# Iterated attention on one core: a round that takes two head pairs instead of one, on all engines

## The chip, the core and the metric

One core of one Trainium2 chip runs the whole kernel. It has TensorE (PE, and PEld for its weight loads), VectorE (DVE), ScalarE (ACT), GpSimd (POOL) and the queue of SyncE. The metric is device time in microseconds (us); lower is better.

## What is computed

A stack of four layers, each with an attention and a feed-forward part, on x of shape (16, 256, 128). Only the attention of the last layer is touched. It has 16 heads of 64 and repeats its own update three times:

```
q, k = layernorm(heads(x @ Wq + bq)), layernorm(heads(x @ Wk + bk)); v = heads(x @ Wv + bv)
def step(carry, _):
    q_cur, converged = carry
    scores = einsum('bhqd,bhkd->bhqk', q_cur, k) / scale
    attn = softmax(scores, axis=-1)
    out = einsum('bhqk,bhkd->bhqd', attn, v)
    diff = norm(out - q_cur)
    q_new = where(converged, q_cur, out)
    return (q_new, converged | (diff < UPDATE_STEPS_EPS)), None
(q_final, _), _ = lax.scan(step, (q, False), None, length=3)
return merged(q_final) @ Wo + bo
```

## The kernel before

`iterated_attention` works in 32 units (NU), each one sequence of 256 tokens and 8 of the 16 heads. A unit is three steps of four head pairs: 12 pairs, 384 in all (NPS). Every engine has its own instruction stream, written out by hand, and works through it in order; semaphores tie the streams together.

A pair p goes through these stages. PE: `scores(p)` (L2456), 12 fp32r matmuls in tiles of 64 rows, into banks S(p, 0) and S(p, 1), which alternate with the pair's parity. DVE: `maxima(p, e)` (L2717), one for each head e of the pair. ACT: `exps(p, e)` (L2588), two exponentials a head with their sums. DVE: `invert(p)` (L2724), both heads' sums in one reciprocal. POOL: `norm(p, e)` (L2873). PE: `turn(p, e)` (L2466), four transposes a head into bank PT(e), of which there is one for each e. ACT and DVE: `move_even` (L2596) and `move_odd` (L2730) copy PT(0) and PT(1) to SBUF. PE: `weigh(p)` (L2481), attention times V in tiles of 64 columns, into O, half of bank 6. ACT: `high(p)` rounds O to fp32r (L2609) and, in the first two steps, copies it in full as well (L2613). DVE: `low(p)` (L2736), what the rounding left. The scores of the same heads in the next step, four pairs on, need high and low.

The order of round p is, on PE: weigh(p-3), turn(p-2), scores(p), and then at most one of the things that belong to a neighbouring unit: a `product` (L2411 to L2413, the projection of x for the next unit, bank M), a `turn_p` (L2428, 4 transposes of projected k or q, right behind turn), or an `out_product` (L2512, the output projection, 12 matmuls, bank M). ACT: exps(p-1), high(p-3), move_even(p-2). DVE: maxima(p-1), the background, invert(p-1), move_odd(p-2), low(p-3). POOL: background, then norm(p-1, 0) and norm(p-1, 1). The background prepares the next unit: `add_bias`, `sum_squares`, `variance`, `newton` (L2683 to L2685), `split_q` (L2694) on DVE; `root`, `lay`, `first_high` and `square_moves` on ACT; `square`, `scale`, `split_k`, and `differ` (L2867, q after a step less q before it) on POOL.

## Time and profile before

| | |
|---|---|
| three runs, median (lowest, highest) | 3319.6 us (3316.22, 3321.14) |
| the profiled execution, first to last instruction | 3317.6 us |
| busy, of the whole span | PE 94%, DVE 78%, ACT 73%, POOL 60% |
| iterated attention | from about 1694 us to the end, half of the span |

One execution was profiled. A page gives the busy time of each engine; behind it stand the chain of work that ended last, the instructions in order of time, and busy times of chosen stretches. Matmuls overlap in the records (each is listed with its fill and drain), so PE's busy share says little on how fast it goes; the distance from the start of one block to the start of the next does.

### The profile page before, as it was taken

The numbers are of one execution on the slowest core, as the hardware profiler recorded it, in microseconds if no ns is written. First come the engines' busy times: TensorE is split into PE (matmuls) and PEld (weight loads), VectorE is DVE, ScalarE is ACT, GpSimd is POOL, SyncE is SP. The second block draws the span as 40 slices with busy tenths as digits, with TensorE's granted clock in tenths as the row PEclk, the third lists the DMA queues.
The fourth block names the chain that finished last, engine by engine and source line by source line (L and its number), as shares of the span: only waits on it lengthen the run. The fifth ranks groups of instructions, "written<-read, shape, count | busy, mean of one in ns | idle before, by whom it ended". The sixth has DMA issues, their size and how long they took to land.

```text
span 3317.6 us, 74521 instructions
## 1 busy us (share of the span) xinstructions
PE 3124.8 (94%) x25143; PEld 2376.0 (72%) x25143; DVE 2572.0 (78%) x5708; ACT 2422.7 (73%) x7208; POOL 1985.8 (60%) x1917
## 2 busy tenths in 40 slices
PE   6999999998699989999989999999999999999997
PEld 5777777766588878788867777777677776776675
DVE  7999999976877775465467787787788788778776
ACT  6888898874355557446448888888888888888885
POOL 3432323322355645425238888888888888888884
PEclk8999999998799989999989999999999999999999
DMA  3122422200000010201100000000000000000000
GB/s 115 63 64 65 127 83 78 80 17 7 1 1 1 1 49 8 71 8 30 33 13 2 2 2 1 2 2 1 2 1 2 1 2 1 2 2 1 2 2 26
DMA packets 67142, 80.44 MB, mean 24 GB/s; under 512 B 7696, under 2 KB 57936, under 8 KB 66512
## 3 DMA queue, kind: packets, MB, share of 16 engines
q1 hardware_dynamic: 65472, 75.27, 7.3%
q8 instruction: 207, 3.39, 0.4%
q14 instruction: 167, 1.37, 0.1%
q10 hardware_dynamic: 1296, 0.41, 0.1%
HBM read 56.79 MB, written 18.87 MB: 23 GB/s over the span
## 4 chain that ended last, share of the span: by engine, by line
PE 45%; POOL 6%; ACT 5%; DVE 4%; issue 3%; DVEq 0%; POOLq 0%; ACTq 0%
PE psum L2466 8%; PE psum L2481 8%; PE psum L2456 8%; PE psum L2512 5%; POOL attn_p L2873 4%; ACT attn_p L2588 3%; PE psum L2411 2%; POOL attn_qf L2867 2%; PE psum L1853 2%; PE psum L1704 2%; PE psum L1946 2%; PE psum L1706 2%; PE psum L1705 2%; PE psum L1753 1%; DVE sb_few L2717 1%
## 5 line engine op out<-in xcount | busy, mean ns | idle before, releaser
L2588 ACT ACTIVATE attn_p<-psum,sb_few 128x256 f32<-128x256 f32 x1536 | 707.8, 476 | 254.4 <-DVE sb_few L2717 249.6
L2873 POOL TENSOR_TENSOR attn_p<-attn_p,sb_few 128x512 f32<-128x512 f32 x768 | 782.4, 1039 | 135.1 <-DVE sb_few L2724 135.1
L2717 DVE TENSOR_REDUCE sb_few<-psum 128x2 f32<-128x512 f32 x768 | 491.4, 681 | 20.7 <-PE psum L2456 20.6
L2466 PEld LDWEIGHTS psum<-sb_kept,attn_p 128*128 128x128 f32 x3072 | 328.8, 141 | 164.3 <-issue 94.2
L2481 PE MATMUL psum<-attn_pt,attn_v 128*64 128x256 f32 x3072 | 416.3, 391 | 31.6 <-DVE attn_ql L2736 27.5
L2466 PE MATMUL psum<-sb_kept,attn_p 128*128 128x128 f32 x3072 | 426.9, 280 | 8.9 <-POOL attn_p L2873 8.9
L537 ACT ACTIVATE sb_a_p<-psum,sb_a_nm 128x256 f32<-128x256 f32 x1024 | 406.8, 499 | 11.3 <-DVE sb_a_nm L464 11.1
L464 DVE TENSOR_REDUCE sb_a_nm<-psum 128x2 f32<-128x512 f32 x512 | 328.4, 683 | 39.3 <-PE psum L358 25.1
L2481 PEld LDWEIGHTS psum<-attn_pt,attn_v 128*64 128x64 f32 x3072 | 192.8, 136 | 179.5 <-issue 58.2
L2588 ACT ACTIVATION_READ_ACCUMULATOR attn_p<-psum,sb_few 128x1 f32 x1536 | 318.5, 207 | 0.0
L2730 DVE COPY attn_pt<-psum 128x512 f32<-128x512 f32 x384 | 262.7, 684 | 71.2 <-PE psum L2466 68.2
L588 POOL TENSOR_TENSOR sb_a_rot<-sb_a_t 128x256 f32<-128x256 f32 x64 | 46.6, 728 | 432.1 <-DVE sb_a_t L444 431.9
L368 PE MATMUL psum<-sb_kept,sb_a_p 128*128 128x128 f32 x2048 | 277.0, 278 | 0.4
L2456 PE MATMUL psum<-attn_kh,attn_qh 64*128 64x256 f32 x1536 | 257.1, 331 | 2.8 <-DVE attn_ql L2694 2.8
L1509 POOL TENSOR_TENSOR experts_hh_low<-experts_h,experts_hh_high 128x512 fp32r<-128x512 f32 x136 | 175.8, 1293 | 133.7 <-ACT experts_hh_high L1534 133.7
L2596 ACT COPY attn_pt<-psum 128x512 f32<-128x512 f32 x384 | 239.3, 623 | 6.5 <-PE psum L2466 6.5
L368 PEld LDWEIGHTS psum<-sb_kept,sb_a_p 128*128 128x128 f32 x2048 | 219.2, 141 | 22.0 <-issue 2.5
L2724 DVE RECIPROCAL sb_few<-sb_few 128x4 f32<-128x4 f32 x384 | 67.8, 177 | 213.8 <-ACT attn_p L2588 211.2
L2456 PE MATMUL psum<-attn_kl,attn_qh 64*128 64x256 f32 x1536 | 216.7, 279 | 0.0
L2456 PE MATMUL psum<-attn_kh,attn_ql 64*128 64x256 f32 x1536 | 215.6, 277 | 0.0
L545 ACT COPY sb_a_pt<-psum 128x512 f32<-128x512 f32 x256 | 153.8, 601 | 63.4 <-PE psum L368 62.7
L1529 ACT ACTIVATE experts_sg<-psum 128x512 f32<-128x512 f32 x136 | 81.4, 598 | 153.8 <-PE psum L1590 145.2
(436 smaller groups left out, 8105.5 us busy)
## 6 DMA issues: line engine op xcount, KB each, us to landing
sb_a_spread<-a_spilled SPq DMA_DIRECT2D x96, 256.0 KB, 3.0
a_spilled<-sb_a_part_hi SPq DMA_DIRECT2D x64, 128.0 KB
a_spilled<-sb_a_part_lo SPq DMA_DIRECT2D x64, 128.0 KB
sb_a_spread<-a_spilled SPq DMA_DIRECT2D x32, 128.0 KB, 2.8
sb_gate_up<-in_L_ffn_Wg SPq DMA_DIRECT2D x32, 128.0 KB
sb_gate_up<-in_L_ffn_Wu SPq DMA_DIRECT2D x32, 128.0 KB
sb_down_w<-in_L_ffn_Wd SPq DMA_DIRECT2D x32, 128.0 KB, 2.5
sb_x<-in_L_attn_x SPq DMA_DIRECT2D x4, 512.0 KB, 7.4
```

Of the source, the lines that this page charges most:

```text
L368: mm = pe.transpose(PT(e)[:, kt * N + t * P:kt * N + (t + 1) * P], Pr[:, p % 3, e, t, kt * P:(kt + 1) * P], c.ident)
L464: dve.tensor_reduce(nm[:, p % 4, e, :], S(p, e).rearrange("p (t n) -> p t n", t=TB), AX.X, ALU.max, negate=True).then_inc(maxed.sem, 1)
L537: ins = act.activation(Pr[:, p % 3, e, t, :], S(p, e)[:, t * N:(t + 1) * N], ACT.Exp, bias=nm[:, p % 4, e, t:t + 1])
L1509: pool.tensor_tensor(hh_low[i % 3][:, :], hh[i % 3][:, :], hh_high[i % 3][:, :].bitcast(F32), ALU.subtract).then_inc(parted.sem, 1)
L2456: mm = pe.matmul(S(p, e)[:, t * N:(t + 1) * N], a_[n][half(e), hp, t * P:(t + 1) * P], b_[u % 2][half(e), hp, :], start=(n_ == 0), stop=(n ...
L2466: mm = pe.transpose(PT(e)[:, kt * N + t * P:kt * N + (t + 1) * P], Pr[p % 3][:, e, t, kt * P:(kt + 1) * P], c.ident)
L2481: mm = pe.matmul(O[half(e), :], V[u % 2][:, kt, h * HD3:(h + 1) * HD3], PTs[p % 2][:, e, kt, :], start=(kt == 0), stop=(kt == TB - 1))
L2588: ins = act.activation(Pr[p % 3][:, e, t, :], S(p, e)[:, t * N:(t + 1) * N], ACT.Exp, bias=nm[:, p % 4, e, t:t + 1], accum_out=rsum[:, p % ...
L2596: act.copy(PTs[p % 2][:, 0, :, :], PT(0).rearrange("p (k n) -> p k n", k=TB)).then_inc(even.sem, 1)
L2717: dve.tensor_reduce(nm[:, p % 4, e, :], S(p, e).rearrange("p (t n) -> p t n", t=TB), AX.X, ALU.max, negate=True).then_inc(maxed.sem, 1)
L2730: dve.tensor_copy(PTs[p % 2][:, 1, :, :], PT(1).rearrange("p (k n) -> p k n", k=TB)).then_inc(odd.sem, 1)
L2873: pool.tensor_tensor(P3, P3, spread(rinv[:, p % 4, e, :], N), ALU.mult).then_inc(normed.sem, 1)
```

## The change

The four streams are rewritten in rounds of two pairs: `TURNS` = 192 rounds, `UR` = 6 to a unit (i = 0 to 5). In round r the pairs b, b+1 with b = 2(r-2) are turned and weighed, the pairs a, a+1 with a = 2(r-1) go through maxima, exponentials and norms, and the scores of b+4, b+5 are made. O gets both halves of bank 6, one for each parity. One ACT copy rounds both pairs' outputs (`highs`), a second keeps them in full (`keep`), and waits for both lows. The sums are inverted head by head. `differ` goes in halves. `normed` and `turned` become a semaphore for each parity of head. PT(0) and PT(1) also take one product and two of the turn_p, so that turn has a further wait in three of six rounds (on add_bias or lay). The diff without the loops that it removes, which stand above, and without the helpers that place the background of ACT, DVE and POOL (which work they place in which round is told below):

```diff
-    O, M = c.banks[6][:, 0:N], c.banks[7]
+    O2 = c.banks[6].rearrange("p (h n) -> p h n", h=2)
+    O = lambda p: O2[:, p % 2, :]
+    M = c.banks[7]
     S = lambda p, e: c.banks[2 * (p % 2) + e]
     PT = lambda e: c.banks[4 + e]
     qslot = lambda u, s: (4 * u + s) % 3
     NPS = NU * ROUNDS
+    TURNS, UR = NPS // 2, ROUNDS // 2
...
-        scored, weighed, inverted = (c.steps(k, NPS) for k in ("scored", "weighed", "inverted"))
-        maxed, exped, normed, turned = (c.steps(k, 2 * NPS) for k in ("maxed", "exped", "normed", "turned"))
+        scored, weighed = (c.steps(k, NPS) for k in ("scored", "weighed"))
+        maxed, exped, inverted = (c.steps(k, 2 * NPS) for k in ("maxed", "exped", "inverted"))
+        normed, turned = ([c.steps(k + e, NPS) for e in ("", "_odd")] for k in ("normed", "turned"))
         even, odd = c.steps("even_moved", NPS), c.steps("odd_moved", NPS)
-        pair_high, pair_low = c.steps("pair_high", NPS), c.steps("pair_low", NPS)
+        pairs_high, pairs_kept, pair_low = c.steps("pair_high", TURNS), c.steps("kept", 2 * TURNS // 3), c.steps("pair_low", NPS)
...
+            def between_turns(u, i):
+                if i == 3 and u:
+                    out_product(u - 1, 2)
+                elif i == 4 and u < NU:
+                    out_product(u, 0)
+                if u + 1 < NU:
+                    if i == 0:
+                        product(u + 1, 1)
+                    elif i == 5:
+                        turn_p(u + 1, 2)
+            def behind_weighing(u, i):
+                if u + 1 < NU:
+                    if i < 3:
+                        product(u + 1, i + 2)
+                    elif i == 3:
+                        turn_p(u + 1, 0)
+                    elif i == 4:
+                        product(u + 1, 5)
+                        turn_p(u + 1, 1)
+                    else:
+                        turn_p(u + 1, 3)
+                if u + 2 < NU and i == 5:
                     product(u + 2, 0)
             def scores(p):
...
             def turn(p, e):
-                pe.wait_ge(*normed(2 * p + e))
+                pe.wait_ge(*normed[e](p))
                 if p:
                     pe.wait_ge(*(even, odd)[e](p - 1))
+                u, i = divmod(p // 2 + 1, UR)
+                if p % 2 == 0 and u + 1 < NU:
+                    if e == 0 and i == 2:
+                        pe.wait_ge(*biased(6 * (u + 1) + 4))
+                    elif e == 0 and i == 4:
+                        pe.wait_ge(*affine(4 * (u + 1) + 1))
+                    elif e == 1 and i == 5:
+                        pe.wait_ge(*affine(4 * (u + 1) + 3))
...
             def weigh(p):
...
                 pe.wait_ge(*even(p))
                 pe.wait_ge(*odd(p))
-                if p:
+                if p and p % 2 == 0:
                     pe.wait_ge(*pair_low(p - 1))
+                    u_, s_, hp_ = place(p - 2)
+                    if s_ < STEPS - 1:
+                        pe.wait_ge(*pairs_kept(4 * u_ + 2 * s_ + hp_ // 2))
                 for kt in range(TB):
                     for e in range(2):
                         h = 2 * hp + e
-                        mm = pe.matmul(O[half(e), :], V[u % 2][:, kt, h * HD3:(h + 1) * HD3],
+                        mm = pe.matmul(O(p)[half(e), :], V[u % 2][:, kt, h * HD3:(h + 1) * HD3],
                                        PTs[p % 2][:, e, kt, :], start=(kt == 0), stop=(kt == TB - 1))
...
+            for r in range(TURNS + 4):
+                u, i = divmod(r, UR)
+                p = 2 * (r - 2)
+                turning = 0 <= p < NPS
+                if turning:
+                    turn(p, 1)
+                    turn(p, 0)
+                between_turns(u, i)
+                if turning:
+                    turn(p + 1, 1)
+                    turn(p + 1, 0)
+                    weigh(p)
+                    weigh(p + 1)
+                behind_weighing(u, i)
+                if r < TURNS:
+                    scores(p + 4)
+                    scores(p + 5)
+                if i == 5:
+                    out_product(u, 1)
+                if r == TURNS + 1:
                     total(0)
...
             def exps(p, e):
                 act.wait_ge(*maxed(2 * p + e))
                 if p >= 3:
-                    act.wait_ge(*turned(2 * (p - 3) + e))
-                if p >= 4 and e == 0:
-                    act.wait_ge(*inverted(p - 4))
+                    act.wait_ge(*turned[e](p - 3))
+                if p >= 4:
+                    act.wait_ge(*inverted(2 * (p - 4) + e))
...
-            def high(p):
+            def highs(p):
                 u, s, hp = place(p)
-                act.wait_ge(*weighed(p))
+                act.wait_ge(*weighed(p + 1))
...
-                ins = act.copy(qh[qslot(u, s + 1)][:, hp, :], O)
+                act.copy(qh[qslot(u, s + 1)][:, hp:hp + 2, :], O2).then_inc(pairs_high.sem, 1)
+            def keep(p):
+                u, s, hp = place(p)
                 if s < STEPS - 1:
+                    act.wait_ge(*pair_low(p + 1))
                     if hp == 0 and u:
                         act.wait_ge(*diff_squared(2 * (u - 1) + 1))
-                    ins = act.copy(qf(u, s + 1)[:, hp, :], O)
-                ins.then_inc(pair_high.sem, 1)
+                    act.copy(qf(u, s + 1)[:, hp:hp + 2, :], O2).then_inc(pairs_kept.sem, 1)
...
+            for r in range(TURNS + 4):
+                u, i = divmod(r, UR)
+                a, b = 2 * (r - 1), 2 * (r - 2)
+                turning, rising = 0 <= b < NPS, 0 <= a < NPS
+                if i == 0 and 0 < u < NU:
+                    first_high(u, 1)
+                if rising:
+                    exps(a, 0)
+                behind_first_exps(u, i)
+                if turning:
+                    move_even(b)
+                if rising:
+                    exps(a, 1)
+                if turning:
+                    move_even(b + 1)
+                if rising:
+                    exps(a + 1, 0)
+                if i == 5 and u + 1 < NU:
+                    lay(u + 1, 2)
+                if turning:
+                    highs(b)
+                if rising:
+                    exps(a + 1, 1)
+                behind_highs(u, i)
+                if turning:
+                    keep(b)
+                behind_keep(u, i)
...
-            def invert(p):
-                dve.wait_ge(*exped(2 * p + 1))
+            def invert(p, e):
+                dve.wait_ge(*exped(2 * p + e))
                 if p >= 4:
-                    dve.wait_ge(*normed(2 * (p - 4) + 1))
-                dve.reciprocal(rinv[:, p % 4, :, :], rsum[:, p % 4, :, :]).then_inc(inverted.sem, 1)
+                    dve.wait_ge(*normed[e](p - 4))
+                dve.reciprocal(rinv[:, p % 4, e, :], rsum[:, p % 4, e, :]).then_inc(inverted.sem, 1)
...
             def low(p):
...
-                dve.wait_ge(*pair_high(p))
-                dve.tensor_tensor(ql[n][:, hp, :], O, qh[n][:, hp, :].bitcast(F32), ALU.subtract).then_inc(pair_low.sem, 1)
+                dve.wait_ge(*pairs_high(p // 2))
+                dve.tensor_tensor(ql[n][:, hp, :], O(p), qh[n][:, hp, :].bitcast(F32), ALU.subtract).then_inc(pair_low.sem, 1)
...
+            for r in range(TURNS + 4):
+                u, i = divmod(r, UR)
+                a, b = 2 * (r - 1), 2 * (r - 2)
+                turning, rising = 0 <= b < NPS, 0 <= a < NPS
+                if rising:
+                    maxima(a, 0)
+                behind_first_maxima(u, i)
+                if rising:
+                    maxima(a, 1)
+                behind_second_maxima(u, i)
+                if turning:
+                    move_odd(b)
+                if rising:
+                    invert(a, 0)
+                    maxima(a + 1, 0)
+                behind_third_maxima(u, i)
+                if turning:
+                    move_odd(b + 1)
+                behind_second_odd(u, i)
+                if rising:
+                    maxima(a + 1, 1)
+                behind_last_maxima(u, i)
+                if rising:
+                    invert(a, 1)
+                if i == 0 and 0 < u < NU:
+                    split_q(u, 1)
+                if turning:
+                    low(b)
+                if rising:
+                    invert(a + 1, 0)
+                if turning:
+                    low(b + 1)
+                if i == 2 and u + 1 < NU:
+                    variance(u + 1, 0)
+                if rising:
+                    invert(a + 1, 1)
+                behind_inverses(u, i)
...
-            def differ(u, s):
-                pool.wait_ge(*pair_low(pair(u, s, GP - 1)))
-                pool.tensor_tensor(qf(u, s)[:, :, :], qf(u, s + 1)[:, :, :], qf(u, s)[:, :, :], ALU.subtract).then_inc(differed.sem, 1)
+            def differ(u, s, k):
+                pool.wait_ge(*pairs_kept(4 * u + 2 * s + k))
+                now, then = qf(u, s + 1)[:, 2 * k:2 * k + 2, :], qf(u, s)[:, 2 * k:2 * k + 2, :]
+                pool.tensor_tensor(then, now, then, ALU.subtract).then_inc(differed.sem, 1)
             def norm(p, e):
-                if e == 0:
-                    pool.wait_ge(*inverted(p))
+                pool.wait_ge(*inverted(2 * p + e))
                 P3 = Pr[p % 3][:, e, :, :]
-                pool.tensor_tensor(P3, P3, spread(rinv[:, p % 4, e, :], N), ALU.mult).then_inc(normed.sem, 1)
+                pool.tensor_tensor(P3, P3, spread(rinv[:, p % 4, e, :], N), ALU.mult).then_inc(normed[e].sem, 1)
...
+            for r in range(TURNS + 4):
+                u, i = divmod(r, UR)
+                a = 2 * (r - 1)
+                rising = 0 <= a < NPS
+                before_norms(u, i)
+                if rising:
+                    norm(a, 0)
+                behind_first_norm(u, i)
+                if rising:
+                    norm(a, 1)
+                    norm(a + 1, 1)
+                if i == 2 and u + 1 < NU:
+                    square(u + 1, 3)
+                elif i == 5:
+                    differ(u, 1, 0)
+                if rising:
+                    norm(a + 1, 0)
```

Background by round i: ACT root behind exps(a, 0) at 3 and 4, lay at 3, 4, 5 and 5, first_high at 5 and 0, square_moves at 1 and 2. DVE split_q at 0 (twice), newton behind maxima(a+1, 0) at 3 and 4, add_bias at 0, 1, 2, 2, 4, 5, sum_squares at 1, 2, 3, 3, step_end at 0, 3, 4. POOL split_k and square at 0, square at 1, two squares and a differ at 2, two scales at 3, two differs and a scale at 4, a scale, split_x (every other unit), split_k and a differ at 5.

PE in a steady unit before, one round with a product; kh, kl, qh, ql are the rounded and left parts of k and q, kept is the identity, pt the turned attention:

```order
L2481 MATMUL psum<-attn_pt,attn_v 64x256 x4
L2466 MATMUL psum<-sb_kept,attn_p 128x128 x8
L2456 MATMUL psum<-attn_kh,attn_qh 128x256 x2
L2456 MATMUL psum<-attn_kl,attn_qh 128x256 x2
L2456 MATMUL psum<-attn_kh,attn_ql 128x256 x2
...
L2411 MATMUL psum<-sb_whi_k,attn_xhi 128x512
```

PE after, round i = 3 and the start of the next:

```order
L2489 MATMUL psum<-sb_kept,attn_p 128x128 x8
L2534 MATMUL psum<-attn_qh,attn_wo 128x256 x2
L2534 MATMUL psum<-attn_ql,attn_wo 128x256
...
L2489 MATMUL psum<-sb_kept,attn_p 128x128 x8
L2507 MATMUL psum<-attn_pt,attn_v 64x256 x8
L2430 MATMUL psum<-sb_kept,attn_wk 128x128 x4
L2471 MATMUL psum<-attn_kh,attn_qh 128x256 x2
...
L2489 MATMUL psum<-sb_kept,attn_p 128x128 x8
```

Turning, weighing and scoring each stand for two pairs in a row now; the scores are 24 matmuls, and the output product stands between the two turns. DVE before, a round with newton, then after, round i = 4:

```order
L2717 TENSOR_REDUCE sb_few<-psum 128x2 x2
L2670 TENSOR_TENSOR attn_wq<-psum,sb_L3bq 128x512
L2683 SCALAR_TENSOR_TENSOR sb_few<-sb_few 128x16
L2684 TENSOR_TENSOR sb_few<-sb_few 128x16
L2685 SCALAR_TENSOR_TENSOR sb_few<-sb_few 128x16
L2724 RECIPROCAL sb_few<-sb_few 128x4
L2730 COPY attn_pt<-psum 128x512
L2736 TENSOR_TENSOR attn_ql<-psum,attn_qh 128x256
```

```order
L2755 TENSOR_REDUCE sb_few<-psum 128x2 x2
L2733 TENSOR_SCALAR sb_few<-sb_few 128x16
L2768 COPY attn_pt<-psum 128x512
L2762 RECIPROCAL sb_few<-sb_few 128x2
L2755 TENSOR_REDUCE sb_few<-psum 128x2
L2737 SCALAR_TENSOR_TENSOR sb_few<-sb_few 128x16
L2738 TENSOR_TENSOR sb_few<-sb_few 128x16
L2739 SCALAR_TENSOR_TENSOR sb_few<-sb_few 128x16
L2768 COPY attn_pt<-psum 128x512
L2784 TENSOR_TENSOR attn_yT<-attn_yT,psum 128x256
```

The first copy of a turned head moved ahead of the maxima of the second pair, and newton stands between the two copies.

## Rows read from the trace of the kernel before

**Rows 1.** Busy us (count) of two units: start:end length, PE PEld DVE ACT POOL, clock.

```profile
2197.07:2246.37 49.30, 47.74 (x412) 34.65 (x410) 39.24 (x84) 41.02 (x143) 42.73 (x41) 1.00 0.01 2
2246.37:2295.67 49.30, 47.74 (x412) 34.66 (x410) 39.30 (x84) 41.02 (x143) 41.70 (x39) 1.00 0.01 2
```

**Rows 2.** The chain that ended last, within that unit: start, us, what.

```profile
2209.23 0.91 PE psum L2456 x12
2210.14 0.43 PE psum L2411
2210.57 0.23 PE psum L2412
...
2211.04 1.01 PE psum L2481 x8
2212.05 1.02 PE psum L2466 x8
...
2221.65 1.63 PE psum L2512 x12
...
2229.16 0.44 PE psum L2428 x4
```

**Rows 3.** Instructions in order of time, PE, a round with turn_p: start, length.

```profile
2228.06 1.09 PE L2466 MATMUL psum<-sb_kept,attn_p 128*128 128x128 f32 x8
2228.99 0.60 PE L2428 MATMUL psum<-sb_kept,attn_wk 128*128 128x128 f32 x4
2229.52 0.39 PE L2456 MATMUL psum<-attn_kh,attn_qh 64*128 64x256 f32 x2
2229.75 0.28 PE L2456 MATMUL psum<-attn_kl,attn_qh 64*128 64x256 f32 x2
2229.86 0.28 PE L2456 MATMUL psum<-attn_kh,attn_ql 64*128 64x256 f32 x2
```

**Rows 4.** The same view, PE, in the expert stage ahead, where every tile is 128*128.

```profile
1635.34 0.48 PE L1704 MATMUL psum<-sb_seT_hi,sb_xlT_hi 128*128 128x512 f32 x1
1635.65 0.40 PE L1705 MATMUL psum<-sb_seT_lo,sb_xlT_hi 128*128 128x512 f32 x1
...
1636.57 0.39 PE L1706 MATMUL psum<-sb_seT_hi,sb_xlT_lo 128*128 128x512 f32 x1
1636.80 1.03 PE L1935 MATMUL psum<-sb_kept,slotmoe_scratch 128*128 128x128 f32 x8
1637.67 1.95 PE L1946 MATMUL psum<-slotmoe_slots,slotmoe_scratch 128*128 128x128 f32 x16
```

**Rows 5.** The same view, ACT, DVE and POOL at the end of a pair's exponentials.

```profile
2212.28 0.48 ACT L2588 ACTIVATE attn_p<-psum,sb_few 128x256 f32<-128x256 f32 x1
2212.64 0.21 ACT L2588 ACTIVATION_READ_ACCUMULATOR attn_p<-psum,sb_few 128x1 f32 x1
2212.73 0.38 ACT L2609 CAST attn_qh<-psum 128x256 fp32r<-128x256 f32 x1
2212.89 0.18 DVE L2724 RECIPROCAL sb_few<-sb_few 128x4 f32<-128x4 f32 x1 [0.80 <-ACT attn_p L2588]
2212.98 0.62 ACT L2596 COPY attn_pt<-psum 128x512 f32<-128x512 f32 x1
2213.16 2.04 POOL L2873 TENSOR_TENSOR attn_p<-attn_p,sb_few 128x512 f32<-128x512 f32 x2
2213.46 1.10 ACT L2619 ACTIVATE attn_qf<-attn_qf 128x1024 f32<-128x1024 f32 x1
```

**Rows 6.** The same view, DVE: a copy, a low, two maxima.

```profile
2204.70 0.69 DVE L2730 COPY attn_pt<-psum 128x512 f32<-128x512 f32 x1
2205.31 0.42 DVE L2736 TENSOR_TENSOR attn_ql<-psum,attn_qh 128x256 fp32r<-128x256 f32 x1
2205.64 1.28 DVE L2717 TENSOR_REDUCE sb_few<-psum 128x2 f32<-128x512 f32 x2
```

**Rows 7.** One line, newton's middle operation: ns shortest/median/longest.

```profile
L2684 DVE TENSOR_TENSOR sb_few<-sb_few x58: 175/604/1034, 1776.3 to 3173.0; 128x16 f32<-128x16 f32 x58
```

More of the change, by code:

```diff
@@ L2902, in pool_program @@
             split_k(0, 1)
[L2903 to L2913 removed]
+            for r in range(TURNS + 4):
[11 more added lines that the diff above has]
+                    square(u + 1, 3)
+                elif i == 5:
+                    differ(u, 1, 0)
+                if rising:
+                    norm(a + 1, 0)
         def sp_program():
```

234 lines of the change are left out of this document (101 added, 133 removed).

## The prediction

> **What bounds the kernel now.** I read the busy times of a stretch first, then the chain that ended last inside it, then PE's instructions in order of time. In iterated attention one unit takes 49.30 us, and the next one the same to the hundredth [rows 1]: a cycle of 12 pairs, 4.11 us each. PE, at the full clock (1.00 is 2.4 GHz), is busy for 47.74 us of it, POOL for 42.73 or 41.70, ACT for 41.02, DVE for 39.24 [rows 1]. PE's figure contains overlap, so its real work has to be read from the distances of its blocks. In the chain [rows 2] the blocks stand end to end: weigh 1.01, turn 1.02, scores 0.91, a product 0.90 (2210.14 to 2211.04), an out_product 1.63, a turn_p 0.44. A unit has 12, 12, 12, 6, 3 and 4 of them: 12 x 2.94 + 6 x 0.90 + 3 x 1.63 + 4 x 0.44 = 47.3 us. PE is the bound, and only 2.0 us of a unit are waits. A change of order that only removed waits could win 2.0 x 32 = 64 us.
>
> **What a change of block costs PE.** The blocks are longer than their matmuls. A score pair of matmuls takes 0.11 to 0.12 (2229.75 to 2229.86) but the first one 0.23 [rows 3]; six steps of 0.12 are 0.71, and the block takes 0.91, so 0.20 go at its two ends. A turn takes 1.02 before scores [rows 2], 0.93 when a turn_p follows (2228.06 to 2228.99), and that turn_p, last before the scores, 0.53 instead of 0.44 [rows 3]: about 0.10 sits where the tile goes from 128*128 to 64*128. Where all tiles are 128*128, eight transposes take 0.87 (1636.80 to 1637.67) and the third matmul of a product 0.23 with the transposes right behind it; only the first fp32r matmul behind fp32 ones is late, 0.31 against 0.23 [rows 4]. So a change of tile costs some 0.15 to 0.20 us, a new block of the same tile nothing, transposes to product 0.08. These blocks begin with semaphore waits too (turn_p waits for scale), so the waits as such are not what costs.
>
> **The change, PE.** Two like blocks in a row save the second one's ends: turn 1.02 + 0.87, weigh 1.01 + 0.87 (I take for eight weighing matmuls what eight transposes take; 1.01 would be the other end), scores 0.91 + 0.71. A round of two pairs: 5.39 instead of 5.88, in six rounds 32.3 us instead of 35.3. Products: one between turns, 0.31 + 2 x 0.23 = 0.77, five between other tiles, 0.90 each: 5.3. turn_p: three beside blocks of their tile, 0.44, one alone between weigh and scores, 0.44 + 0.15: 1.9. out_product: two between turns, 12 x 0.12 + 0.08 = 1.50, one between scores and turn, 1.56: 4.6. Sum 44.0 us, against 47.3. If weighing saved nothing it would be 44.9.
>
> **The other engines.** DVE gets 12 more reciprocals a unit, each of four numbers fewer; the row has 0.18 and the next operation starts later by that at most [rows 5]: up to 2.2, DVE then works 41.4. ACT makes 6 copies of 512 columns for 12 roundings of 256, and 4 for 8 full ones; a copy of 512 takes 0.48 to the next instruction (2212.98 to 2213.46), one of 256 0.25 [rows 5]: nothing to a few tenths saved, 41.0 stays as a bound. POOL keeps its 24 norms of 1.02 [rows 5] and the rest; differ in halves costs between nothing and a start-up each, I take nothing: 42.2 on average [rows 1]. All four then lie between 41 and 44, so waits decide what is left.
>
> **The waits, laid out by hand.** Take round i = 1 with 0 at the start of turn(b, 1). I use, from start to next start, exponentials of a head 0.90, ACT copy 0.48, DVE copy 0.61, low 0.33, maxima 0.60 [rows 5, 6]; results count when they are finished (0.62, 0.69, 0.42) plus 0.04 to 0.10 for the semaphore (2212.85 to 2212.89, 2213.07 to 2213.16 in rows 5).
> - PE turns b in 0.93. DVE copies the odd head at 0.60, done 1.29. PT(1) is single, so turn(b+1, 1) can start only at 1.38: PE waits 0.45. This wait is new in kind: before, scores stood between two turns.
> - ACT: exps(a, 0) from 0.02, the even copy at 1.03, exps(a, 1) 1.51, second even copy 2.41, done 3.03, exps(a+1, 0) 2.89. PE: second turns end at 2.34, weigh(b) to 3.24, weigh(b+1) to 4.19, no wait.
> - highs at 4.29, done 4.91; exps(a+1, 1) to 5.77; low(b) done 5.36, low(b+1) 5.84. PE: product to 5.09, scores(b+4) at once, scores(b+5) behind exps(a+1, 1) at 5.89: no wait. The round ends at 6.70.
> - In rounds i = 2 to 5 the scores also need the low of the same round (they belong to the next step of the heads just weighed; before, that low was a round old). At i = 2 they start at 5.46 instead of 5.09, the round ends at 7.08.
> - i = 3 has root on ACT and newton on DVE in front of the copies, and only a turn_p (0.59) between weigh and scores: 8.1 us, 0.7 of it waits. i = 4 and 5 have 1.33 us of other blocks there and an out_product: 8.2 and 8.75, with 0.0 and 0.1 of waits. i = 0 has a product between the turns: 7.0, none.
> POOL, laid out the same way, starts its first norm 1.4 us into round 1 and ends its last 1.4 us into the next, ahead of turn(b+1, 0), which needs it at 1.81; it is late nowhere by more than 0.2.
> Waits sum to 2.1 us a unit. This layout has no slack for hand-overs that I count at their shortest, so I take 2.4: **46.4 us a unit** instead of 49.3. For 31 units (the cycle is not there in the first rounds) 31 x 2.9 = 90 us less; rounds of two pairs fill and drain the pipeline about one pair later, 4.1 us more. Span 3317.6 - 90 + 4 = 3232; the median of the runs stands 2.0 above the profiled span, so **3234 us**.
>
> **Rivals.**
> (A) The forecast, with waits from 1 to 5 us a unit: 45.0 to 49.0, that is 3191 to 3315; below 48 us most of it.
> (B) The engines run further apart than in my layout and only the PT wait of rounds 1 and 2 is left, 0.9: 44.9 us a unit, 3187; if that is hidden as well, 44.0, 3159. For it: POOL and ACT are 2 us below. Against it: the low of the same round.
> (C) Slower: a round becomes a serial chain. PT is single, both weighs stand behind four copies, highs waits for the second weigh, low for highs, the next scores for low. Without any background the chain is 0.50 + copy 0.83 + 0.96 + copy 0.77 + weigh 0.96 + highs, low and semaphores 1.33 + scores 1.62 = 7.0 us. Each hand-over can find ACT inside a head's exponentials (0.90) or DVE inside a maximum or newton (0.6 to 1.4). It decides from 49.3/6 = 8.2 us a round on average, 1.2 us more than the chain; with two such misses a round, about 8.8 us, a unit takes 52.8 and the kernel 3319.6 + 31 x 3.5 + 4 = 3432. For it: three copies, highs and newton stand in fixed order behind exponentials. Against it: my layout finds one miss in a round, and rounds 4, 5 and 0 have other PE work in just these places.
> (D) The ends of blocks cost because of the waits and not the tile. Then PE still works 47.3 us a unit and the new waits come on top: 49.3 to 50.5, 3324 to 3361. Against it: turn to turn_p at no cost [rows 3], and the expert stage [rows 4].
> (E) POOL holds DVE up. Newton's middle operation works on 16 numbers and takes from 175 to 1034 ns, 604 in the middle [rows 7]; a norm takes 1.02 [rows 5], so at its longest it sits out a whole POOL instruction. It stands ahead of the second odd copy now, so that weigh(b+1) and all behind it wait with it; at 1.03 each time two units' halves cost 2 x 0.43 = 0.9 us a unit, 27 us: 3261. The Trainium skill (SBUF — State Buffer, Who interferes with whom) says that a VectorE instruction with two SBUF inputs and a GpSimd instruction that reads SBUF exclude each other for the whole instruction; by that rule, the trace agrees, and the reciprocals, maxima and lows, with one SBUF input at most, are free of it.
>
> **How the numbers follow.** A 0.74, B 0.09, C 0.08, D 0.04, E 0.05. The predicted time is A's, 3234. The range 3180 to 3300 holds B's first case, E, and A up to 48.5 us a unit; outside are C, D, B's last case and the upper end of A, together about 0.18. A measurement of this kernel tells about 0.2%, 6.6 us, from no change. Faster by more than that: A but for its end (0.72), B and E: 0.86. Within it: 0.04, from A's end and D. Slower: C and part of D, 0.10.
>
> **What would show it.** Right: turns of two pairs 1.9 us and scores of two 1.6 us from start to start; PE with a gap of about 0.45 ahead of the second odd turn in rounds 1 and 2, and a short one ahead of scores in rounds 2 and 3; a unit at 46 to 47 us, POOL about 42 of it. Wrong: two-pair blocks as long as twice the single ones (D); PE waiting for copies ahead of weigh or turn in most rounds (C); newton at 1.0 us each time (E); POOL without idle time and PE waiting for norms, which no case above has.

## The result and the profile after

| | before | after |
|---|---|---|
| runs, median (lowest, highest), us | 3320.37 (3316.22, 3321.47) | 3286.57 (3283.64, 3290.42) |
| the profiled execution, us | 3317.6 | 3287.4 |
| ratio of the times, 95% interval | | 0.9904 (0.989 to 0.9918) |

The change makes the kernel 33.8 us faster. The forecast was 86 us faster: the direction was right, and the time lies inside the range, but less than half of the gain came.

The busy times of the whole span:

```profile
PE 3049.8 (93%) x25143; PEld 2380.6 (72%) x25143; DVE 2669.5 (81%) x6092; ACT 2430.9 (74%) x6888; POOL 1995.5 (61%) x1981
```

Two units of the steady part, in the view of [rows 1] (length, then PE, PEld, DVE, ACT, POOL, and the clock; here for both units together, since they differ by 0.3 us):

```profile
2254.28:2350.47 96.19, 90.48 (x815) 69.57 (x816) 84.84 (x191) 82.55 (x264) 84.99 (x83) 1.00 0.01 2
```

A unit takes 48.1 us instead of 49.3 [rows 1], at the same full clock. 31 x 1.2 = 37 less, and 33.8 was measured, so that some 3 us are left for filling and draining; 4 had been taken for it. What has to be explained is the unit: 48.1, and not 46.4.

The chain that ended last, two rounds of it, in the view of [rows 2]. It shows that PE's blocks cost what the forecast said:

```profile
2254.28 1.88 PE psum L2507 x16
...
2257.05 1.69 PE psum L2471 x24
...
2264.29 1.69 PE psum L2471 x24
2265.98 1.02 PE psum L2489 x8
2267.01 1.43 PE psum L2534 x12
2268.43 0.87 PE psum L2489 x8
```

Sixteen weighing matmuls take 1.88 us, where two single blocks took 2 x 1.01 [rows 2], 24 of scores 1.69 in this chain and 1.62 or 1.63 from their start to the next block's (2264.29 to 2265.91, 2281.78 to 2283.41), where they took 2 x 0.91, and the output projection between two turns takes 1.50 (2266.76 to 2268.27) instead of 1.63.

So the round has to be looked at. Below is the distance from the first turn of a round to the first turn of the next, read off PE's instructions in order of time, each a mean of two neighbouring units (they differ at i = 0 by 0.4 us and elsewhere by 0.06 at most):

| us | i = 0 | 1 | 2 | 3 | 4 | 5 | unit |
|---|---|---|---|---|---|---|---|
| laid out by hand in the prediction | 7.0 | 6.70 | 7.08 | 8.1 | **8.2** | 8.75 | 45.8 |
| after | 7.38 | 7.02 | 7.24 | 8.15 | **9.35** | 8.96 | 48.1 |

Half of the excess sits in one round. PE's instructions there, in order of time (start, length, what; in brackets the idle time ahead and who ended it):

```profile
2276.42 1.04 PE L2489 MATMUL psum<-sb_kept,attn_p 128*128 128x128 f32 x8
2277.38 1.08 PE L2507 MATMUL psum<-attn_pt,attn_v 128*64 128x256 f32 x8
2279.43 1.08 PE L2507 MATMUL psum<-attn_pt,attn_v 128*64 128x256 f32 x8 [0.97 <-DVE attn_pt L2768]
```

The second turn starts at 2276.42, its odd half is done half a microsecond later, and the first weigh runs at once. The second weigh then stands still for the odd copy (L2768). The same view of DVE, and of POOL beside it:

```profile
2276.36 0.16 DVE L2737 SCALAR_TENSOR_TENSOR sb_few<-sb_few 128x16 f32<-128x16 f32 x1
2276.55 0.90 DVE L2738 TENSOR_TENSOR sb_few<-sb_few 128x16 f32<-128x16 f32 x1
2277.49 1.20 DVE L2739 SCALAR_TENSOR_TENSOR sb_few<-sb_few 128x16 f32<-128x16 f32 x1
2278.61 0.68 DVE L2768 COPY attn_pt<-psum 128x512 f32<-128x512 f32 x1
```

```profile
2276.36 1.06 POOL L2969 TENSOR_TENSOR attn_p<-attn_p,sb_few 128x512 f32<-128x512 f32 x1
2277.39 1.26 POOL L2964 TENSOR_TENSOR attn_qf<-attn_qf 128x512 f32<-128x512 f32 x1
2278.77 1.04 POOL L2950 TENSOR_TENSOR attn_wq<-attn_wq,sb_few 128x512 f32<-128x512 f32 x1
```

Newton's three operations work on 16 numbers each. The second ends at 2277.45, POOL's norm at 2277.42; the third at 2278.69, its half of differ at 2278.65. From the first to the copy pass 2.25 us. All 60 executions of each of the three in iterated attention (ns shortest/median/longest):

```profile
L2737 DVE SCALAR_TENSOR_TENSOR sb_few<-sb_few x60: 155/438/996, 1787.1 to 3190.3; 128x16 f32<-128x16 f32 x60
L2738 DVE TENSOR_TENSOR sb_few<-sb_few x60: 174/538/906, 1788.1 to 3190.5; 128x16 f32<-128x16 f32 x60
L2739 DVE SCALAR_TENSOR_TENSOR sb_few<-sb_few x60: 174/684/1201, 1788.3 to 3191.4; 128x16 f32<-128x16 f32 x60
```

These medians hide two kinds. At i = 3 the first operation takes 0.99 (0.71 in one unit) and the other two 0.17 or 0.18 each; at i = 4 the three take 0.16, 0.90 and 1.20, in every unit. Before, it was the middle operation alone: 29 of its 58 executions took 1.03 and 29 took 0.17, so the 604 ns of [rows 7] is the mean of the two values in the middle, and no execution took it. The last one was never held then:

```profile
L2685 DVE SCALAR_TENSOR_TENSOR sb_few<-sb_few x58: 174/174/176, 1777.3 to 3173.2; 128x16 f32<-128x16 f32 x58
```

At i = 4 two instructions of POOL back to back, norm and half a differ, now seem to hold one operation each.

At i = 0 DVE is late in the same manner, at `split_q`, and with it `step_end` (L2784), for which PE's product waits:

```profile
2290.93 1.80 DVE L2748 TENSOR_TENSOR attn_ql<-attn_qf,attn_qh 128x512 fp32r<-128x512 f32 x1
2292.65 0.68 DVE L2755 TENSOR_REDUCE sb_few<-psum 128x2 f32<-128x512 f32 x1
2293.25 0.41 DVE L2784 TENSOR_TENSOR attn_yT<-attn_yT,psum 128x256 f32<-128x256 f32 x1
```

```profile
2293.71 0.50 PE L2413 MATMUL psum<-sb_whi_k,attn_xhi 128*128 128x512 f32 x1 [0.31 <-DVE attn_yT L2784]
```

At i = 1 PE waits for the single PT(1), as forecast, only a little longer. PE and the copy that it waits for:

```profile
2299.95 1.09 PE L2489 MATMUL psum<-sb_kept,attn_p 128*128 128x128 f32 x8
2301.48 1.07 PE L2489 MATMUL psum<-sb_kept,attn_p 128*128 128x128 f32 x8 [0.44 <-DVE attn_pt L2768]
```

```profile
2300.64 0.70 DVE attn_pt L2768
2301.34 0.14 issue
```

From the first turn to the copy 0.69, the copy 0.70, to the second turn 0.14: 1.53 us from turn to turn. The layout had 0.60, 0.69 and 0.09: 1.38.

### The profile page after: what moved, and what is told of

Same layout as the page of the kernel before. It is cut to its first block, busy times and chain, and to the rows that moved or that the text cites. A ratio compares the mean times of both kernels' runs of the same rounds, so it can differ in the third digit from the quotient of the medians.

```text
span 3287.4 us, 75219 instructions
## 1 busy us (share of the span) xinstructions
PE 3049.8 (93%) x25143; PEld 2380.6 (72%) x25143; DVE 2669.5 (81%) x6092; ACT 2430.9 (74%) x6888; POOL 1995.5 (61%) x1981
## 4 chain that ended last, share of the span: by engine, by line
PE 37%; DVE 9%; POOL 8%; issue 5%; ACT 3%; DVEq 0%; POOLq 0%; ACTq 0%
PE psum L2507 9%; PE psum L2489 7%; PE psum L2471 6%; POOL attn_p L2969 4%; DVE attn_pt L2768 2%; DVE sb_few L2755 2%; PE psum L1853 2%; PE psum L1704 2%; PE psum L1946 2%; ACT attn_p L2613 2%; PE psum L1706 2%; PE psum L1705 2%; PE psum L1753 2%; PE psum L2534 1%; PE psum L2413 1%
## 5 line engine op out<-in xcount | busy, mean ns | idle before, releaser
L2969 POOL TENSOR_TENSOR attn_p<-attn_p,sb_few 128x512 f32<-128x512 f32 x768 | 796.0, 1050 | 174.9 <-DVE sb_few L2762 173.8
L2613 ACT ACTIVATE attn_p<-psum,sb_few 128x256 f32<-128x256 f32 x1536 | 720.2, 479 | 61.1 <-DVE sb_few L2755 61.0
L2755 DVE TENSOR_REDUCE sb_few<-psum 128x2 f32<-128x512 f32 x768 | 508.0, 679 | 12.1 <-PE psum L2471 6.7
L2489 PE MATMUL psum<-sb_kept,attn_p 128*128 128x128 f32 x3072 | 412.4, 277 | 32.9 <-DVE attn_pt L2768 29.2
L2507 PE MATMUL psum<-attn_pt,attn_v 128*64 128x256 f32 x3072 | 385.0, 387 | 30.4 <-DVE attn_pt L2768 30.4
L2507 PEld LDWEIGHTS psum<-attn_pt,attn_v 128*64 128x64 f32 x3072 | 203.0, 136 | 157.3 <-issue 76.3
L2768 DVE COPY attn_pt<-psum 128x512 f32<-128x512 f32 x384 | 263.9, 687 | 34.3 <-PE psum L2489 30.1
L2621 ACT COPY attn_pt<-psum 128x512 f32<-128x512 f32 x384 | 223.7, 583 | 67.7 <-PE psum L2489 63.2
L2471 PE MATMUL psum<-attn_kh,attn_qh 64*128 64x256 f32 x1536 | 242.7, 312 | 31.4 <-DVE attn_ql L2774 30.0
L2774 DVE TENSOR_TENSOR attn_ql<-psum,attn_qh 128x256 fp32r<-128x256 f32 x384 | 156.7, 414 | 130.1 <-ACT attn_qh L2634 130.0
L2471 PEld LDWEIGHTS psum<-attn_kh,attn_qh 64*128 64x128 f32 x1536 | 146.1, 186 | 96.3 <-DVE attn_ql L2774 70.2
```

Source lines behind the costliest of these rows:

```text
L2471: mm = pe.matmul(S(p, e)[:, t * N:(t + 1) * N], a_[n][half(e), hp, t * P:(t + 1) * P], b_[u % 2][half(e), hp, :], start=(n_ == 0), stop=(n ...
L2489: mm = pe.transpose(PT(e)[:, kt * N + t * P:kt * N + (t + 1) * P], Pr[p % 3][:, e, t, kt * P:(kt + 1) * P], c.ident)
L2507: mm = pe.matmul(O(p)[half(e), :], V[u % 2][:, kt, h * HD3:(h + 1) * HD3], PTs[p % 2][:, e, kt, :], start=(kt == 0), stop=(kt == TB - 1))
L2613: ins = act.activation(Pr[p % 3][:, e, t, :], S(p, e)[:, t * N:(t + 1) * N], ACT.Exp, bias=nm[:, p % 4, e, t:t + 1], accum_out=rsum[:, p % ...
L2621: act.copy(PTs[p % 2][:, 0, :, :], PT(0).rearrange("p (k n) -> p k n", k=TB)).then_inc(even.sem, 1)
L2755: dve.tensor_reduce(nm[:, p % 4, e, :], S(p, e).rearrange("p (t n) -> p t n", t=TB), AX.X, ALU.max, negate=True).then_inc(maxed.sem, 1)
```

## The experiments

The theory after this reading (T1): DVE stands between PE's blocks, and what POOL makes it wait there sets i = 4 and part of i = 0. Its rivals: the delay at i = 4 would be replaced by the next late thing as soon as it is gone, or it is not a matter of POOL but of the length of the chain of hand-overs. Each kernel was timed beside the kernel before, and the ratio is to that. The kernel before itself took 3321.0, 3318.4 and 3313.9 us in the three groups of runs (3320.4 beside the change), so that a difference in us from the change's 3286.6 can be off by some 6 us.

**newton_free.** The change, with newton replaced from the second unit on by three operations of the same size that read one SBUF tensor each; the refinement of the reciprocal root is left out there.

```diff
+                if u:
+                    own(dve.reciprocal(t_[:, :, :], v_[:, :, :]))
+                    own(dve.reciprocal(t_[:, :, :], v_[:, :, :]))
+                    dve.reciprocal(t_[:, :, :], v_[:, :, :]).then_inc(refined.sem, 1)
+                    return
```

> The changed kernel with newton's three operations replaced by three reciprocals of the same 16 numbers, each with one SBUF input; the refinement of the inverse root is left out. Theory 1 (a POOL instruction holds up DVE operations with two SBUF inputs, and in round i = 4 the second odd copy and weigh(b+1) wait for that, 0.97 us of PE a unit): newton of round 4 shrinks from 2.25 to about 0.7 us, PE's wait ahead of weigh(b+1) goes, 0.9 us a unit, 28 us: about 3258 us. Theory 2 (the gain went to the waits that belong to the round itself, single PT and the low of the same round, and they would fill in behind newton): under 0.3 us a unit, 3278 to 3287 us.

3247.95 us (3245.11 to 3250.02), ratio 0.978 (0.9766 to 0.9795): 38.6 us faster than the change, where 28 had been expected. The round i = 4 takes 8.16. Each of the three operations takes 0.24 or 0.25 us, though POOL's norm runs beside them. The rival is out by 30 us. Since these operations are also of another kind, this kernel alone can't say that it is POOL that newton waits for; differ_late asks that.

**newton_late.** Nothing left out; the second newton of a unit moves behind the second odd copy.

```diff
-                if u + 1 < NU and i in (3, 4):
-                    newton(u + 1, i - 3)
+                if u + 1 < NU and i == 3:
+                    newton(u + 1, 0)
...
                     step_end(u, 0)
+                    if u + 1 < NU:
+                        newton(u + 1, 1)
```

> The changed kernel with the second newton of each unit (round i = 4) moved on DVE from behind the third maxima to behind the second odd copy and step_end. All work is kept. Theory 1: the copy is no longer behind it, weigh(b+1) does not wait; the fourth maxima come later instead, and exponentials of head (a+1, 1) with them, about 0.2 us a unit: 3262 us. Theory 2: 3280 to 3290 us.

3250.18 us (3247.43 to 3251.95), ratio 0.9785 (0.9769 to 0.9802). That is 12 us faster than expected, and moving one newton is worth nearly what freeing both is. PE at i = 4, where both weighs run without a break:

```profile
2263.54 1.04 PE L2489 MATMUL psum<-sb_kept,attn_p 128*128 128x128 f32 x8
2264.51 1.95 PE L2507 MATMUL psum<-attn_pt,attn_v 128*64 128x256 f32 x16
```

The round takes 8.17 us, all others stay within 0.02: 9.35 - 8.17 = 1.18, and 31 x 1.18 = 36.6, beside the 36.4 measured. It is more than the 0.97 that PE stood idle, from which the expectation was worked out: two weighs without a break take 1.88 (2264.51 to the product at 2266.39), and with the break 3.07 (2277.38 to 2280.45 in the change), 1.19 more. The newton at i = 3 costs about 0.1 (8.14 us with it, 8.03 in newton_free), though its first operation is held as well.

**differ_late.** Newton stays; instead POOL's second half of differ at i = 4 moves to ahead of its last norm of the round.

```diff
-                elif i == 4 and u < NU:
-                    differ(u, 0, 1)
...
+                elif i == 4 and u < NU:
+                    differ(u, 0, 1)
                 if rising:
                     norm(a + 1, 0)
```

> The changed kernel with newton where it is, and on POOL the second half of differ of round i = 4 moved from between the first two norms to ahead of the last. All work is kept. Theory 1 (POOL's back-to-back instructions with SBUF inputs hold newton up): POOL is idle when newton's last operation comes, newton ends about 1 us earlier, weigh(b+1) with it: 3255 to 3265 us. Rival (newton is long for a reason on DVE itself, and newton_late gained only because it moved): no change, 3283 to 3290 us.

3272.24 us (3270.74 to 3278.09), ratio 0.9865 (0.985 to 0.988): 14 us, where T1 had 22 to 32. DVE in that round:

```profile
2275.20 0.16 DVE L2737 SCALAR_TENSOR_TENSOR sb_few<-sb_few 128x16 f32<-128x16 f32 x1
2275.40 0.90 DVE L2738 TENSOR_TENSOR sb_few<-sb_few 128x16 f32<-128x16 f32 x1
2276.34 0.18 DVE L2739 SCALAR_TENSOR_TENSOR sb_few<-sb_few 128x16 f32<-128x16 f32 x1
2276.43 0.68 DVE L2768 COPY attn_pt<-psum 128x512 f32<-128x512 f32 x1
```

With no second POOL instruction there, the last operation takes 0.18 instead of 1.20, and the round 8.33: the third operation's wait is POOL's doing. The second still takes 0.90, beside the norm. Half of the gain is given back one round on. The chain there:

```profile
2280.17 1.04 POOL attn_p L2969
2281.21 1.24 POOL attn_qf L2964
2282.45 1.01 POOL attn_p L2969
2283.45 0.04 issue
2283.50 0.66 PE psum L2489 x4
```

The moved differ (2281.21) stands ahead of the last norm, and the turn of the next round waits for that norm: i = 5 takes 9.40 instead of 8.96, and i = 0 7.49 instead of 7.38. Sum: -1.02 + 0.44 + 0.11 = -0.47 a unit, 31 of them 14.6. The layout said that POOL is late nowhere by more than 0.2; 1.28 us more ahead of that norm is too much.

**splitq_late.** The change, with `split_q(u, 0)` at i = 0 moved from behind the first maximum to behind the last.

```diff
             def behind_first_maxima(u, i):
-                if i == 0 and 0 < u < NU:
-                    split_q(u, 0)
...
             def behind_last_maxima(u, i):
+                if i == 0 and 0 < u < NU:
+                    split_q(u, 0)
```

> The changed kernel with split_q(u, 0) moved in round i = 0 from between the first two maxima to behind the last maxima. All work is kept. Theory 1 (it is held up by POOL, 1.8 us instead of 0.8, and step_end and the product between the turns wait for it): the 0.3 to 0.5 us that PE waits ahead of that product go, 10 to 15 us: about 3274 us. Theory 2: within 3 us of 3287.

3307.71 us (3305.13 to 3309.67), ratio 0.996 (0.9946 to 0.9975): 21 us slower than the change, a miss. The chain at i = 0:

```profile
2109.39 0.60 DVE sb_few L2755
2109.99 0.88 DVE attn_ql L2748
2110.88 0.07 DVE sb_few L2762
2110.95 1.38 DVE attn_ql L2748
2112.33 0.04 issue
2112.38 1.00 PE psum L2471 x12
```

Both halves of split_q now end together, and the round's scores need them. The round takes 8.11 instead of 7.38, 31 x 0.73 = 23. The copies had waited for split_q, but the scores wait for it too. So this run doesn't show what the held split_q costs in its old place.

**newton_late_splitq_mid.** newton_late, and `split_q(u, 0)` one maximum later, behind the second and still ahead of step_end.

```diff
             def behind_second_maxima(u, i):
+                if i == 0 and 0 < u < NU:
+                    split_q(u, 0)
                 if i == 0 and u:
                     step_end(u - 1, 1)
```

> newton_late, and split_q(u, 0) of round i = 0 moved from between the first two maxima to behind the second, ahead of step_end, where DVE otherwise waits for the out_product. The second maxima come 1 us earlier, step_end up to 0.5 us earlier: PE's wait of 0.33 us ahead of the product between the turns shrinks or goes. Against newton_late (3250 us) 0.2 to 0.4 us a unit less: 3238 to 3245 us. If the wait is made up by POOL's norms behind it: 3248 to 3252 us.

3248.44 us (3241.41 to 3249.68), ratio 0.9786 (0.977 to 0.9801): nothing that can be told from newton_late, as in the second of the two cases expected. Round i = 0 takes 7.01 and 7.57 in turn, where it took 7.60 and 7.20: one unit gains 0.6 and the next loses nearly 0.4, which leaves 0.1 a unit.

**splitq_mid_differ_early.** The same, and the first half of differ that POOL makes at i = 5 moves to i = 1 of the next unit.

```diff
+                elif i == 1 and u:
+                    differ(u - 1, 1, 0)
...
-                elif i == 5:
-                    differ(u, 1, 0)
```

> newton_late_splitq_mid, and the half of differ of round i = 5 (the step's first two pairs) moved to round i = 1 of the next unit, where POOL has 5.4 us of work in a 7 us round instead of 8.4 to 9.5 in 9. If POOL's load in rounds 4 to 0 is what the chain runs through next (it does in newton_late for some 20 us of each 94), and if that differ holds split_q up: 0.3 to 0.6 us a unit less, 3222 to 3232 us. If PE's own chain is the bound there: as newton_late_splitq_mid.

3241.32 us (3236.32 to 3247.24), ratio 0.977 (0.9753 to 0.9786). The size was missed (10 to 20 had been expected, 7 came, about as much as the spread), and i = 0 comes down to 7.01 and 7.33. It is the fastest of all kernels run, 45 us faster than the change, with all of the work kept.

**invert_pair.** The change, with the sums inverted for both heads of a pair at once, in the place where the second head's was.

```diff
             def invert(p, e):
-                dve.wait_ge(*exped(2 * p + e))
+                if e == 0:
+                    return
+                dve.wait_ge(*exped(2 * p + 1))
...
-                dve.reciprocal(rinv[:, p % 4, e, :], rsum[:, p % 4, e, :]).then_inc(inverted.sem, 1)
+                dve.reciprocal(rinv[:, p % 4, :, :], rsum[:, p % 4, :, :]).then_inc(inverted.sem, 1)
...
             def norm(p, e):
-                pool.wait_ge(*inverted(2 * p + e))
+                pool.wait_ge(*inverted(p))
```

> The changed kernel with one part undone: the sums of a pair are inverted in one reciprocal behind the second head's exponentials, not head by head. DVE has 12 reciprocals a unit fewer (1 us). If POOL's early start of norm(a, 0) matters (POOL waited 9.5 us in two units for reciprocals as it is), its norms end later and PE waits ahead of the turns: 3300 to 3330 us. If only DVE's load matters: 3270 to 3280 us.

3539.28 us (3537.06 to 3542.46), ratio 1.0659 (1.0643 to 1.0675), 200 us above both ranges, a miss. POOL's instructions in order of time:

```profile
2258.58 1.28 POOL L2968 TENSOR_TENSOR attn_qf<-attn_qf 128x512 f32<-128x512 f32 x1
2263.14 1.04 POOL L2973 TENSOR_TENSOR attn_p<-attn_p,sb_few 128x512 f32<-128x512 f32 x1 [3.27 <-DVE sb_few L2766]
2264.14 1.29 POOL L2968 TENSOR_TENSOR attn_qf<-attn_qf 128x512 f32<-128x512 f32 x1
2265.38 1.05 POOL L2954 TENSOR_TENSOR attn_wq<-attn_wq,sb_few 128x512 f32<-128x512 f32 x1
2266.38 3.04 POOL L2973 TENSOR_TENSOR attn_p<-attn_p,sb_few 128x512 f32<-128x512 f32 x3
2269.37 1.05 POOL L2954 TENSOR_TENSOR attn_wq<-attn_wq,sb_few 128x512 f32<-128x512 f32 x1
```

POOL stands idle for 3.27 us, then has four norms and its background to do in a row, and the turns wait for it. A round of the change gives POOL 8 us for 7 us of work, so a start 3 us late can't be made good. In the 96 us from 2254 us on POOL waits 22.3 us so, 10 times. A unit takes 56.4 us on average, 7.1 more than before, 1.2 a round. The round has become a serial chain, as in rival C, though at another link than those named there; that is read from this trace, and no further run tests it. Part of the loss is TensorE's clock. The same stretch has a granted clock of 0.96, where the change has 1.00:

```profile
2254.00:2350.00 96.00, 82.12 (x709) 62.79 (x709) 68.52 (x140) 70.34 (x223) 73.34 (x72) 0.96 0.01 2
```

PE had stood idle for 2.25 us up to 2284.49 and then worked for some 1.2 us when the clock fell: from 2286 to 2289 us it is 0.50, the level of 1.2 GHz. The 16 transposes there take 3.3 us (2286.45 to 2289.75), where a first and a second turn take 1.9. A clock of 0.96 makes a unit longer by 0.04 x 56.4 = 2.3 us at most (an estimate), so that up to a third of the 7.1 is the clock's. Another place for the pair's reciprocal was not tried.

**before_invert_by_head.** The kernel before, with that part alone.

```diff
-                dve.wait_ge(*exped(2 * p + 1))
+                dve.wait_ge(*exped(2 * p + e))
...
-                dve.reciprocal(rinv[:, p % 4, :, :], rsum[:, p % 4, :, :]).then_inc(inverted.sem, 1)
+                dve.reciprocal(rinv[:, p % 4, e, :], rsum[:, p % 4, e, :]).then_inc(inverted.sem, 1)
```

> The kernel before with one part of the change alone: the sums of a pair inverted head by head, in two reciprocals at the place of the one. norm(p, 0) still waits for the second head's exponentials nearly always, since invert(p, 0) stands in the same place behind both maxima; DVE gets 1 us a unit more. Expected: within 0.2% of the kernel before, 3314 to 3326 us; a gain above 0.3% would say that the inversion alone was part of the win.

3313.5 us (3310.22 to 3321.39), ratio 0.999 (0.9981 to 1.0): within 0.2%. Alone it is worth next to nothing; in the new order, giving it up costs 253 us. Its page also prices it on DVE, 2572.0 before and here

```profile
PE 3118.4 (94%) x25143; PEld 2378.0 (72%) x25143; DVE 2634.1 (79%) x6092; ACT 2416.4 (73%) x7208; POOL 1967.6 (59%) x1917
```

that is 62 / 31 = 2.0 us a unit for 12 reciprocals, as forecast (2.2 at most).

**maxima_first.** The change, with the third maximum of a round ahead of both odd copies.

```diff
+                if rising:
+                    maxima(a + 1, 0)
                 if turning:
                     move_odd(b)
                 if rising:
                     invert(a, 0)
-                    maxima(a + 1, 0)
```

> The changed kernel with one edit on DVE: maxima(a+1, 0) moves from behind the first odd copy of a round to ahead of it, so that three maxima stand ahead of the copies; nothing is left out. The copy that frees PT(1) then starts one maximum (0.60 us from start to start) later. Theory 1 (PT is single and DVE is not ahead of PE, so the place of the maxima between the copies carries the gain): in rounds i = 1 and 2 PE waits 0.6 us more, in i = 0 and 5, which have 0.8 and 0.6 us of other work between the turns, some 0.4 to 0.6, in i = 3 and 4 (1.5 us between the turns) nothing: about 2.2 us a unit, 31 x 2.2 = 68 us, 3355 (3330 to 3380). Rival (DVE reaches the copies early and waits for PE there, as its idle time of 11 us in two units would allow): the same as the changed kernel, 3287.

3343.53 us (3338.18 to 3343.71), ratio 1.0084 (1.0069 to 1.0099): 57 us slower than the change, inside the range of Theory 1, and slower than before. PE at i = 1:

```profile
2270.36 1.09 PE L2489 MATMUL psum<-sb_kept,attn_p 128*128 128x128 f32 x8
2272.32 1.07 PE L2489 MATMUL psum<-sb_kept,attn_p 128*128 128x128 f32 x8 [0.87 <-DVE attn_pt L2768]
```

From turn to turn 1.96 instead of 1.53. By rounds, against the change: i = 0 to 5 +0.41, +0.40, +0.43, -0.10, +0.14, +0.51, in all 1.8 a unit (2.2 had been expected).

**maxima_behind.** The change, with the third maximum behind both odd copies.

```diff
-                    maxima(a + 1, 0)
                 behind_third_maxima(u, i)
                 if turning:
                     move_odd(b + 1)
+                if rising:
+                    maxima(a + 1, 0)
```

> The changed kernel with one edit on DVE: maxima(a+1, 0) moves from ahead of the second odd copy to behind it, so that the copies stand together; nothing is left out. Theory 1 (each place in the round is full): the second copy ends about 2.4 us into the round, the maximum 0.7 later, and exps(a+1, 0), which starts at 2.9 now, waits some 0.3 us; highs, low and the next scores follow: 0.3 us in rounds i = 1, 2 and 3, 0.9 a unit, 31 x 0.9 = 28 us, 3315 (3300 to 3330). Where newton stands ahead of the copy (i = 3 and 4) the maximum is late by that as well, which could double it. Rival (ACT has the slack for it): the same as the changed kernel, 3287, or slightly faster, since newton and the copy at i = 4 come 0.6 us earlier: down to 3287 - 31 x 0.6 = 3268.

3338.96 us (3332.93 to 3342.53), ratio 1.0073 (1.0057 to 1.009): 52 us slower than the change, nearly twice the expected 28 and above its range. ACT at i = 1, ahead of the exponentials of the third head:

```profile
2269.39 0.58 ACT L2621 COPY attn_pt<-psum 128x512 f32<-128x512 f32 x1
2270.28 0.47 ACT L2613 ACTIVATE attn_p<-psum,sb_few 128x256 f32<-128x256 f32 x1 [0.30 <-DVE sb_few L2755]
```

Those 0.30 go on to highs, low and scores: +0.57, +0.24, +0.11, +0.28, +0.12, +0.40 for i = 0 to 5, 1.7 a unit. Of the three places tried, the one between the copies is the best for PE and ACT, and it is worth more than the whole gain of the change.

The rounds of all kernels that tell T1 from its rivals (us, means of two units):

| us | i = 0 | 1 | 2 | 3 | 4 | 5 | unit |
|---|---|---|---|---|---|---|---|
| after | 7.38 | 7.02 | 7.24 | 8.15 | 9.35 | 8.96 | 48.1 |
| newton_free | 7.38 | 7.02 | 7.24 | 8.03 | 8.16 | 8.96 | 46.8 |
| newton_late | 7.40 | 7.02 | 7.25 | 8.14 | 8.17 | 8.96 | 46.9 |
| differ_late | 7.49 | 7.02 | 7.25 | 8.14 | 8.33 | 9.40 | 47.6 |
| splitq_late | 8.11 | 6.99 | 7.25 | 8.15 | 9.35 | 8.96 | 48.8 |
| splitq_mid_differ_early | 7.17 | 6.99 | 7.24 | 8.14 | 8.17 | 8.96 | 46.7 |

## Why the prediction was right and wrong

**The step that failed** is the sum of the waits, and in it one term: at i = 4 the layout has 8.2 us and 0.0 of waits. The prediction doesn't print what it counted there for newton, but rival E's 0.43 is 1.03 less the 0.60 of [rows 7], so the layout had the middle operation at 0.60 and the last one unheld. With that, newton would take some 0.92 us from its start to the copy (an estimate: the measured 2.25, less 0.30 for the second operation and 1.03 for the third). It takes 2.25, and 1.18 of the difference lie bare on PE's path: 37 of the 53 us that the forecast was off. newton_late shows it: with newton out of the way the round has 8.17, the 8.2 of the layout, and the kernel comes to 3250, 16 us above the forecast.

**Rival E** named this mechanism and priced it at 0.43 for each of two newtons, 27 us, with a chance of 0.05. It was wrong in three ways. It let one operation be held, where at i = 4 two are, the last one for 1.20. It charged both newtons alike; the one at i = 3 costs about 0.1 (newton_free), the one at i = 4 1.18. And it took the median of before as the usual case, though no execution of before took it: one newton of each unit had its middle operation at 1.03, the other at 0.17. Whether POOL has an instruction running is no matter of chance in a cycle written by hand, it comes out the same in every unit (i = 4 takes 9.34 to 9.38 in all 28 units from 1800 to 3150 us). In the new order newton at i = 4 stands beside half a differ, a norm and half a differ with no gap between them. The Trainium skill (SBUF — State Buffer, Who interferes with whom) gives the rule that a VectorE instruction with two SBUF inputs and a GpSimd one that reads SBUF exclude each other for their whole length. The trace agrees: the two ends above lie 0.03 and 0.04 us behind POOL's, the third operation is short when POOL stands idle (differ_late), and newton_free, with one SBUF input each, has no such wait.

**Its own sums** differ a little: the six rounds of the layout come to 45.8 us, while the work of 44.0 (44.1 by its terms) and the waits of 2.1 come to 46.1. The 46.4 that it took is above both.

**The other excess**, 1.1 us a unit, is in small pieces: at i = 0 0.4 (split_q held by POOL, then step_end late; the layout had no wait there), at i = 1 0.3 (0.15 of it the wait for PT(1), 0.6 us and not 0.45, the rest block ends), at i = 5 0.2, at i = 2 0.16, at i = 3 0.05. Of it 0.6 was allowed for, since the forecast took 46.4 and not the 45.8 of the layout; the other 0.5 is the 16 us by which newton_late stays above 3234.

**What held.** PE's work: two-pair blocks of 1.88, 1.62 to 1.69 and 1.8 to 1.9 us (0.85 to 0.93 for a first turn with another block right behind it, 0.97 to 1.00 for a second) against 1.88, 1.62 and 1.89. Rival D, which had the ends of the blocks come from the waits, is out. Waits stand where the layout had them: PT(1) in rounds 1 and 2, low ahead of the scores at i = 2 (0.25) and i = 3 (0.55). Round i = 3 came out to 0.05 us. ACT, 82.55 in two units against 2 x 41.02 [rows 1], saved nothing by the wider copies. The two halves of a differ take 1.28 us each, 2.56 together, and the whole one before 2.36, or 2.90 where it stood beside split_q (half of the 60 executions each). So the halves cost POOL some 0.2 us a differ, 0.4 a unit, for which the prediction took nothing; POOL works 42.5 us a unit where it had 42.2. Rival C did not come, but its chance of 0.08 was low: three small edits of DVE's order, invert_pair and the two of the maxima, each end slower than before, and the first of them passes C's 3432.

**What stays open.** Whether the 0.6 us between the turns at i = 1 and 2 can be filled was not tried. And the split of the 0.4 us at i = 0 between split_q and step_end is read from the trace alone; moving split_q by itself only shifts it. With half a differ moved away as well (splitq_mid_differ_early) i = 0 comes to 7.01 in every other unit, the 7.0 of the layout. How much of invert_pair's 253 us is POOL's late start, and how much the clock or the waits of the other engines, was not tested.

## What to carry to other kernels

When work moves in a fixed cycle, write down for each small VectorE instruction on the path that reads two tensors in SBUF what GpSimd runs in that very moment. The median of a duration that depends on that neighbour says nothing on the new place; here it was a duration that never occurred. Two small operations of 16 numbers ahead of a copy cost this kernel more than the change brought; moving one call took them off the path. And where every engine works 85% or more of a round, as here, try each step of the order against its two neighbours: a maximum moved by one place cost 52 to 57 us.

## What the runs showed of the hardware

- A VectorE operation on 128x16 numbers, 0.17 us by itself, took 0.90 and 1.20 us beside GpSimd instructions of 1.06 and 1.26 us (after, i = 4), 0.99 in after at i = 3, 1.03 before. Two GpSimd instructions in a row held two operations, one each. A 128x512 `split_q` with two SBUF inputs took 0.88 to 1.80 us. A reciprocal of 128x2, beside the same GpSimd work, kept to 147 to 168 ns in all of 724 executions.
- A GpSimd instruction can be held in turn: beside the split_q of 1.80 us a norm took 1.49 instead of 1.04, beside one of 1.07 half a differ took 1.74 instead of 1.28 (2243.48 us).
- The cost of changing the tile, some 0.2 us for a pair of changes on TensorE, was an inference from the blocks of before. The blocks of two pairs came out as it said, within 0.07 us each; no run changes the tile alone.
- In invert_pair the granted clock of TensorE fell to 0.50 (1.2 GHz) for some 3 us after PE had stood idle for 2.25 us and worked again for 1.2; 16 transposes took 3.3 us there instead of some 1.9.
